# Two bias rows of a graph network's node stage: added on GpSimd's prepared rows, or by a rank-two product on TensorE

## What is computed

```
x = _layernorm(h + o, ln1_g, ln1_b)
f = jax.nn.relu(x @ W1 + b1) @ W2 + b2
return _layernorm(x + f, ln2_g, ln2_b)
```

## Time and profile before

| | |
|---|---|
| median of 3 runs | 2845.94 us (2825.38 to 2848.08) |
| the profiled execution | 2843.35 us, its span 2841.2 us |
| granted TensorE clock, mean of the span | 0.889 |
| busy: TensorE, VectorE, ScalarE, GpSimd | 2310.8, 1811.9, 1010.0, 1152.9 us |
| L335, L338 | 160 matmul passes each (two for each product), from 121.8 to 1017.5 us |

### The profile page before, as it was taken

The page is one execution under the profiler, slowest core; times in us unless marked ns, Lnnn a source line. Parts: engine busy times, 40 slices in busy tenths (PEclk is TensorE's granted clock), DMA queues, the critical chain, the costliest instruction groups (busy, mean ns, idle before and its releaser), DMA issues.

```text
span 2841.2 us, 29188 instructions
## 1 busy us (share of the span) xinstructions
PE 2310.8 (81%) x9582; PEld 1207.5 (42%) x9582; DVE 1811.9 (64%) x3780; ACT 1010.0 (36%) x1735; POOL 1152.9 (41%) x869
## 2 busy tenths in 40 slices
PE   8589999999999859999056766639999798398887
PEld 4245555555545435545022122114444554154465
DVE  2999887888887872245763443363566748647753
ACT  2134545455445442121152222231111132256554
POOL 1777445363767264320626556531120201133222
PEclk9799999999999989999568888769899698599988
DMA  6324333433344146325645565571120202223221
GB/s 196 92 76 117 119 101 115 114 116 116 104 123 114 51 117 164 100 76 172 193 144 141 149 170 137 155 215 46 44 71 17 77 10 58 72 71 81 56 56 52
DMA packets 214465, 298.37 MB, mean 105 GB/s; under 512 B 99951, under 2 KB 100446, under 8 KB 212957
## 3 DMA queue, kind: packets, MB, share of 16 engines
q1 hardware_dynamic: 108116, 213.88, 25.1%
q0 software_dynamic: 106240, 83.12, 11.8%
HBM read 171.56 MB, written 160.65 MB: 117 GB/s over the span
## 4 chain that ended last, share of the span: by engine, by line
PE 56%; DVE 19%; issue 7%; POOL 6%; DMA 6%; ACT 4%; SPq 1%; POOLq 0%; DVEq 0%; ACTq 0%
PE bank L1939 8%; PE bank L321 7%; PE bank L938 7%; PE bank L305 6%; POOL arena L1532 4%; PE bank L2535 3%; PE bank L297 3%; DVE Bd L592 3%; PE bank L918 3%; DMA arena<-y_table,ids 2%; PE bank L312 2%; POOL arena L1030 2%; PE bank L313 2%; PE bank L2418 2%; DVE st L605 2%
## 5 line engine op out<-in xcount | busy, mean ns | idle before, releaser
L1030 POOL DMA_INDIRECT arena<-x_table,idd x120 | 150.5, 1254 | 649.8 <-DVE arena L2205 155.8
L305 PE MATMUL bank<-arena 128*125 128x512 f32 x640 | 292.8, 612 | 15.3 <-DMA ident<-ident_in 8.8
L1586 PE MATMUL bank<-arena 125*125 125x512 f32 x360 | 213.2, 725 | 106.5 <-DMA arena<-y_table,ids 98.5
L1939 PE MATMUL bank<-arena 128*125 128x512 f32 x640 | 292.3, 611 | 1.4 <-DVE Md L2159 0.7
L1532 POOL DMA_INDIRECT arena<-y_table,ids x180 | 228.6, 1270 | 155.7 <-DMA y_table<-arena 103.6
L321 PE MATMUL bank<-arena 128*125 128x512 f32 x640 | 278.5, 593 | 2.1 <-ACT arena L486 1.8
L1760 DVE SCALAR_TENSOR_TENSOR arena<-arena,v,bank 125x512 f32<-125x512 f32 x180 | 134.4, 747 | 193.9 <-PE bank L1586 180.6
L748 POOL TENSOR_TENSOR arena<-arena,rowv 125x512 f32<-125x512 f32 x80 | 100.3, 1286 | 356.4 <-DVE arena L676 314.3
L946 ACT ACTIVATE arena<-bank 128x500 f32<-128x500 f32 (+1 forms) x210 | 114.9, 589 | 293.5 <-PE bank L918 144.0
L938 PE MATMUL bank<-arena 128*125 128x512 f32 x480 | 208.7, 593 | 0.0
L1637 ACT ACTIVATE bank<-arena 125x512 f32<-125x512 f32 x180 | 107.5, 600 | 269.0 <-DVE arena L1760 256.3
(11 more groups left out here) (398 smaller groups left out, 4331.2 us busy)
## 6 DMA issues: line engine op xcount, KB each, us to landing
y_table<-arena SPq DMA_DIRECT2D x36, 896.0 KB
p_table<-arena SPq DMA_DIRECT2D x25, 896.0 KB
z_table<-arena SPq DMA_DIRECT2D x25, 896.0 KB
x_table<-arena SPq DMA_DIRECT2D x25, 896.0 KB
arena<-x_cols SPq DMA_DIRECT2D x20, 1000.0 KB
arena<-x SPq DMA_DIRECT2D x20, 896.0 KB
out<-arena SPq DMA_DIRECT2D x20, 896.0 KB
x_by_src<-arena SPq DMA_DIRECT2D x5, 896.0 KB
```

What stands on the lines that cost most here:

```text
L305: i = nc.tensor.matmul(b[0:P, :], xT[:, k, j * P:(j + 1) * P], W1r[:, k, :], start=k == 0, stop=k == KC - 1)
L1030: nc.gpsimd.indirect_dma_start(out=dst, out_offset=None, in_=table, in_offset=bass.IndirectOffsetOnAxis(ap=idx, axis=0), bounds_check=limi ...
L1586: nc.tensor.matmul(bank[t % RING1][0:P, :], Ss[:, t, :], V1[:, t, :], start=False, stop=True, skip_group_check=True).then_inc(P_sum, 1)
L1939: i = nc.tensor.matmul(b[0:P, :], fT[:, k, j * P:(j + 1) * P], W[:, k, :], start=k == 0, stop=k == KC - 1)
```

## The change

The products of L338 are gone, and the four small loads of their two rows with them. A row `ffn_b` (ln1_b and b2 broadcast to 125 partitions by two loads, added once by VectorE at the end of step 0) is added by GpSimd to U, between L750 and L754. L748 now counts on a new semaphore `tm`, and the addition counts on `tg`, for which VectorE's L655 waits. The rows of ones stay for other uses.

```diff
@@ sp_second_loads
-            for dst, src in ((wleft, w_left), (w2x4[:, 0, :], w_ffn[:, 0:D])):
+            for dst, src in ((wleft, w_left), (w2x4, w_ffn)):
                 sp.dma_start(dst, src).then_inc(s_w2, 16)
-            for j in range(TG):
-                sp.dma_start(w2x4[32 * j:32 * j + 2, 1, :], w_ffn[0:2, D:2 * D]).then_inc(s_w2, 16)
@@ pe_step
                 for j in range(TG):
-                    nc.tensor.matmul(bs[j][0:P, :], f1T[32 * j:32 * j + 32, :], w2x4[32 * j:32 * j + 32, 0, :],
-                                     start=True, stop=False)
-                for j in range(TG):
-                    nc.tensor.matmul(bs[j][0:P, :], ones4[32 * j:32 * j + 2, :], w2x4[32 * j:32 * j + 2, 1, :],
-                                     start=False, stop=True).then_inc(NR_ps, 1)
+                    nc.tensor.matmul(bs[j][0:P, :], f1T[32 * j:32 * j + 32, :], w2x4[32 * j:32 * j + 32, :],
+                                     start=True, stop=True).then_inc(NR_ps, 1)
@@ pool_step
                 for j in range(TG):
-                    nc.gpsimd.tensor_tensor(U[:, j, :], T[1 - par][:, j, :], row(R_LN1G), ALU.mult).then_inc(B["tg"], 1)
+                    nc.gpsimd.tensor_tensor(U[:, j, :], T[1 - par][:, j, :], row(R_LN1G), ALU.mult).then_inc(B["tm"], 1)
                 for j in range(TG):
                     nc.gpsimd.tensor_scalar(T[1 - par][:, j, :], T[1 - par][:, j, :], q2[1 - par][:, j:j + 1], None,
                                             ALU.mult).then_inc(B["wq"], 1)
+                for j in range(TG):
+                    pool.wait_ge(B["tm"], 4 * nB + j + 1)
+                    nc.gpsimd.tensor_tensor(U[:, j, :], U[:, j, :], ffn_b, ALU.add).then_inc(B["tg"], 1)
@@ SyncE, step 0
                     sp.dma_start(rowv[:, R_LN1G:R_END, :], rows[R_LN1G:R_END].partition_broadcast(P)).then_inc(s_rows, 16)
+                    for dst, r in ((ffn_b, R_LN1B), (ffn_b2, R_L2B2)):
+                        sp.dma_start(dst, rows[r].partition_broadcast(P)).then_inc(s_rows, 16)
@@ VectorE, behind its step 0
+                    if s == 0:
+                        dve.wait_ge(s_rows, 16 * 3)
+                        nc.vector.tensor_tensor(ffn_b, ffn_b, ffn_b2, ALU.add).then_inc(wp_rdy, 1)
@@ GpSimd, ahead of its step 1
-                    pool.wait_ge(s_rows, 16)
+                    pool.wait_ge(s_rows, 16 * 3)
+                    pool.wait_ge(wp_rdy, 3)
```

More of the change, by code:

```diff
@@ L105, in gnn_kernel @@
         kd = at(23848, [2, 2 * ET], P)
-        w2x4 = at(35499, [2, D])
+        w2x4, ffn_b = at(35499, [D]), at(34907, [D], P)
+        ffn_b2 = at(23928, [D], P)
         WM0, maps, ones4 = at(36523, [128]), at(36651, [M_END, 128]), at(37675, [P])
@@ L123, in gnn_kernel @@
         B = {k: sem("B_" + k) for k in
-             "tg wq w bn ag sc rt rc ug z3 bn3 ag3 sc3 rt3 rc3 x3".split()}
+             "tm tg wq w bn ag sc rt rc ug z3 bn3 ag3 sc3 rt3 rc3 x3".split()}
         C = {k: sem("C_" + k) for k in
@@ L345, in pe_step @@
                 if isinstance(s, int) and s == 1:
-                    pe.wait_ge(s_w2, 16 * 7)
+                    pe.wait_ge(s_w2, 16 * 3)
                 pe.wait_ge(A["t"], 4 * s)
@@ L1865, in sp_L2 @@
             sp.dma_start(RD[:, :, :], RSd.rearrange("(t p) q -> p t q", p=P)).then_inc(rec_back, 16)
-            sp.wait_ge(s_w2, 16 * 9)
+            sp.wait_ge(s_w2, 16 * 5)
             sp.dma_start(C3[:, 0:M_NDC, :], maps_d[:, 0:M_NDC * 128]).then_inc(w2_in, 16)
@@ L2915, in step @@
                 if isinstance(s, int):
+                    if s == 0:
+                        dve.wait_ge(s_rows, 16 * 3)
+                        nc.vector.tensor_tensor(ffn_b, ffn_b, ffn_b2, ALU.add).then_inc(wp_rdy, 1)
                     if s == W_STEP:
                         dve.wait_ge(NT_sb, st_.count("w_g", 1))
-                        dve.wait_ge(s_rows, 16)
-                        dve.wait_ge(s_w2, 16 * 7)
+                        dve.wait_ge(s_rows, 16 * 3)
+                        dve.wait_ge(s_w2, 16 * 3)
                         nc.vector.tensor_copy(maps[:, M_ND1, :], wcol(W_ND1, 128))
@@ L3001 @@
     w32[:, V_F2:V_END] = np.tile(np.concatenate([f2, s2, a["L3_gnn_W_f1"]], axis=1), (4, 1))
-    w_ffn = np.concatenate([np.tile(a["L2_gnn_W2"], (4, 1)), np.zeros((128, D), f32)], axis=1)
-    w_ffn[0, D:], w_ffn[1, D:] = a["L2_gnn_ln1_b"], a["L2_gnn_b2"]
+    w_ffn = np.tile(a["L2_gnn_W2"], (4, 1))
     g2T = a["L3_gnn_W_g2"][:, 0:128].T
```

## The result

The changed kernel takes 2883.35 us (median of 4 runs, 2874.75 to 2901.97) against 2844.93 us before (4 runs): a ratio of 1.0158, 95% interval 1.009 to 1.0227. That is slower, since the interval lies above 1, and by 38 us where 17 were forecast. The profiled execution took 2874.75 us, its span is 2873.0.

The account below looks back on a forecast made before the run. TensorE was taken to bound the loop, with VectorE's route only 1.4 us behind. 9.5 (steady) + 3.7 (first) + 4 (last) = 17 us on 2843.35 gave 2860.5, as median 2863 us; own range 2852 to 2876.

Parts of the forecast that it names:

- wider range: Whole kernel: 2835 to 2892 us, from a partial gain to long waits in nearly all steps.
- second rival: Loop steps: L704 or L711 waits to the train's end, 2879 us for half the steps, 2895 for all; chance 0.2.
- TensorE's part: Loop steps: dropping the products of L338 takes 0.97 us off TensorE per step, at most 19 us over twenty steps.
- Where the train lies: Loop steps: L754 moves into L741's place, L741 4.9 us later over VectorE's L725, L726 and L728, making VectorE's route longer.
- the price of a blocked L704: Loop steps of the other parity: L704 waits for one L754 instruction, about 1.2 us more, making the step 47.0 us.
- steady part: Loop steps: 0.45 or 1.65 us longer in turn, 8.4 us for eight, 1 for a late one; +9.5 us.
- The clock: TensorE in the loop: left out as the clock showed 1.00; a fall in the new gaps would make the sum wrong.
- First steps: Up to step 3: loads 2.0, counting passes 3.5, a blocked L704 1.2, L671 relieved by 3; sum +3.7 us.
- Last steps: Where records are built: four small VectorE copies take 1.2 us each, +4 us; the four steps after taken as 0.
- The 0.97 us come out: Loop steps: small operations slip in between the new instructions and TensorE sets the step; 2827 to 2843 us, chance 0.2.
- Nothing happens: Whole kernel: TensorE spends the products' time anyway and port costs cancel; within 5 us of 2846, chance 0.1.
- The blocked operations wait to the end of a longer train: Loop steps: L704 gets in only after 9.8 us of GpSimd instructions, making a step 49.5 us, 4.1 longer; chance 0.2.

Follow-up runs that it names:

- e1_no_bias: The changed kernel without its four additions on GpSimd, both bias rows left out of the result: 2838.19 us, ratio 0.9997 to the kernel before.
- e8_drained: The changed kernel with each instruction of GpSimd's trains L737, L750 and L753 waiting for the end of the one before it: 2862.85 us, ratio 1.01.
- e9: The changed kernel with L737 held until VectorE's first L608 of the step, and pauses between the instructions of GpSimd's trains: 2845.36 us, ratio 0.9991.
- e10: The kernel before with its L741 held until VectorE's first L612 of the step, and pauses between the instructions of GpSimd's trains: 2821.88 us, ratio 0.9922.
- e5_apart: The changed kernel with, from step 4 on, L753 moved into the next step behind the first L608, and L737 behind L655: 2841.94 us, ratio 1.001.
- e2_both: The kernel before with the two loads and four GpSimd additions of a row of zeros added, TensorE's products kept: 2888.16 us, ratio 1.0187.

## Why the prediction was right in direction and short in size

The kernel became slower, as forecast, but 2883 us lies above the forecast's own range of 2852 to 2876 and within the wider range that made room for the second rival. In the node stage the trace shows 42.3 us for the forecast's 17: 32.5 in steps 4 to 13 (forecast 9.5), 4.4 before them (3.7) and 5.5 behind (4).

**TensorE's part.** Forecast 0.97 us per step, measured 0.86 (45.41 to 44.55 us, e1_no_bias). The mechanism was right, and so was the claim that VectorE would take the gain away: of the nine steps 5 to 13 two reach 45.3 and 45.4 us, none less.

**Where the train lies.** Right: L753 in L737's old place, and L737 over L722 and L724, which take 0.88 and 1.30 us in steps 5, 7 and 11, as forecast (0.8 to 1.3); in steps 6, 10 and 13 only L722 is long, and in the others L700 has already waited to the train's end, or nearly. And in six of the nine steps TensorE stands still ahead of its first gate product for 2.4 to 3.7 us (forecast 1 to 3), released by ScalarE's evacuation.

**The term that was mis-sized** is the price of a blocked L704 (now L700) in a loop step. I took "one instruction of L754, about 1.2 us more", with steps of 45.8 and 47.0 us in turn and +9.5 us for the steady part. It was +24.1 us in steps 5 to 13 and +8.4 in step 4. In steps 4, 8, 9 and 12 L700 waited 10.63, 5.60, 5.80 and 7.57 us, three of them to the end of the whole L737 train. That is my second rival, which had 0.2 and 2879 us for half of the steps. The forecast loop exists: it is that of e8_drained from step 7 on, where every wait is one instruction, with steps of 46.6 us (forecast mean 46.4). Its ratio of 1.010 is to a kernel before without pauses, which gain time there too.

The evidence was there. The L704 of the earlier trace rows waited from 679.72 to 682.31, and L741 ended at 677.31 + 4.97 = 682.28: it, too, had waited to the end of a train, which was then only two instructions away; so had the L704 of steps 7, 9 and 11. I read it as a number of instructions instead of as a place. The Trainium skill ("SBUF — State Buffer", Who interferes with whom) says that whichever of the two issues first has the shared ports for a whole instruction and the other blocks. e8_drained agrees: 1.32 us at the most in these steps, and a GpSimd instruction takes 1.24. Without pauses the rule is short of what the runs show, nine instructions in step 4; what the lone instruction costs is one thing, who gets the ports at its end another. I had let that rule count against the rival.

**The clock.** I left it out, and named it as something that could spoil the sum. It did, by nearly half of what steps 5 to 13 lost. Windows of TensorE in the changed kernel (busy, granted clock, DMA share, GB/s), behind the idle time of step 6 and behind that of step 12:

```profile
350.13:353.13 3.00, 0.91 (x9) 1.00 0.84 189
353.13:356.13 3.00, 2.70 (x4) 0.52 0.96 335
```

```profile
637.40:640.40 3.00, 0.92 (x9) 1.00 0.83 197
640.40:643.40 3.00, 2.70 (x7) 1.00 0.96 298
```

After 2.39 us of idle time in step 6 TensorE runs at 0.52, the 1.2 GHz level, for some 3 us; after 2.38 us in step 12 it stays at 2.4 GHz. From L311 to the last a_o2 bank (fourth L615) the one takes 376.98 - 353.43 = 23.55 us, the other 662.66 - 640.70 = 21.96:

```profile
353.43 2.03 PE L311 MATMUL bank<-arena,ws 128*128 128x500 f32 x2 [2.39 <-ACT arena L482]
```

```profile
376.98 0.69 DVE L615 TENSOR_TENSOR arena<-arena,bank 125x512 f32<-125x512 f32 x1 [2.75 <-PE bank L320]
...
662.66 0.69 DVE L615 TENSOR_TENSOR arena<-arena,bank 125x512 f32<-125x512 f32 x1 [2.74 <-PE bank L320]
```

So 1.6 us for each such step. Steps 6, 8, 9, 10 and 13 show it, 8 of the 24.1 us, and step 4 does. Step 5 begins at the lower level, behind 5.16 us of idle time that the 10.63 us of L700 brought, and comes to its first transposes (L296) 2.9 us later than step 6 does (10.92 against 8.04 us from its start), so some 11 of the 24.1 us are clock:

```profile
287.50:292.50 5.00, 0.01 (x1) 0.93 0.01 2
292.67:295.67 3.00, 3.00 (x9) 0.50 0.18 16
295.67:298.67 3.00, 3.00 (x5) 0.51 0.92 285
298.67:301.67 3.00, 3.00 (x8) 1.00 0.23 49
```

Gaps of 1.8 us or less (e8_drained, step after step) left the clock at 1.00. A gap's length alone doesn't decide: behind 2.33 us in step 4 of e8_drained the clock stayed at 1.00 too, behind 2.08 us in step 4 of the changed kernel it fell. These waits on VectorE were thus paid twice, once as a gap and once as slow products behind it.

**First steps.** Forecast +3.7, measured +4.4, but by other terms, so the agreement is luck. The window of 28 to 42 us moved 223 GB/s, not 255, and the counting began 1.2 us later (78.11 against 76.92), not 2.0; the step 2 product came 4.7 us later, which the "5 us later" of the forecast meets. Step 2, with +1.2 forecast, is 4.1 us shorter, as L704 had waited 5.54 us there and L700 takes 0.55. Step 3 is 3.8 us longer: the three microseconds that L671 was to give back there didn't come, it takes 8.12 us for four, hardly less than the 8.52 of the earlier trace rows.

```profile
78.11 0.35 DVE L588 SCALAR_TENSOR_TENSOR Bd<-Sd,kfc,arena 125x125 uint8<-125x125 f32 x1
...
197.40 8.12 DVE L667 SCALAR_TENSOR_TENSOR arena<-arena,nb,rowv 125x512 f32<-125x512 f32 x4
```

**Last steps.** The record copies were forecast at +4 us, and step 14 is 5.5 us longer; more operations in the records' row take 1.2 us each (L1095 to L1103), and L1109 2.39 us for two copies:

```profile
761.81 2.39 DVE L1109 COPY Md<-kfc 125x20 f32<-125x20 f32 x2
...
781.15 4.79 DVE L608 TENSOR_SCALAR sr<-mv 125x4 f32<-125x4 f32 x1
```

For steps 15 to 18 I had taken 0; they came to -3.8, and the L612 of the earlier trace rows met the train again, with 4.79 us. Step 19, which I had not named, is 4.8 us longer. In both kernels most of these steps are longer than they need be, through waits that fall here or there. e9 and e10 show what the additions cost when the longest of these are gone: 15 us in steps 14 to 20, where GpSimd also writes the records.

**The rivals.** "The 0.97 us come out" is refuted for this placement, and shown to be true for another (e5_apart, 44.55 us in every loop step). "Nothing happens" is refuted by the interval. "The blocked operations wait to the end of a longer train" happened in three of the ten loop steps, and in a fourth (step 4) nearly to its end. **The chances**: 0.67 stood on a change under 1% and it was 1.6%; 0.28 stood on slower by more.

**What stays open** is what decides, in a train without pauses, whether VectorE gets in at the next boundary (steps 5 to 7, 10, 11, 13) or only later (4, 8, 9, 12). The pauses show what removes the long wait, not what chooses between the two. Where in a GpSimd instruction the small operation starts doesn't decide it alone: in e2_both L705 (L700) starts 1.08 us into one in steps 8 and 10, and takes 0.23 and 7.56 us. Nor does a long wait always last to the end of a train: besides the L700 of step 4, L608 there waits 8.32 us (258.88 to 267.20) and gets in between L744 and L746, which follow without a pause.

## What to carry to other kernels

Before work is put on GpSimd, ask which small VectorE operations on the critical chain will find it busy, and price each at the whole run of back-to-back GpSimd instructions that may follow, not at one. A hold that starts the train behind the chain's small operations, or a wait between its instructions, costs one line and is worth trying by itself: here it gave 0.5 to 0.8% without the change, as much as the change could have given at its best (19 us). Give the kernel before the same hold when the two are compared; otherwise its gain is booked to the change. And where the bounding engine would get gaps like those here (2 to 5 us), look at its granted clock behind them before calling the gap the whole price.

## What the hardware showed beyond expectation

- A VectorE operation on 125x4 numbers, 0.17 us alone, took up to 13.3 us beside GpSimd's trains (e2_both, step 4), and a counting pass of some 1.3 us took 11.48 us in the kernel before. RECIPROCAL on the same tiles, in the same place, stayed at 0.16 to 0.18 us, and so did additions with a PSUM bank as an input (0.69 us).
- A wait for the instruction before it, though it costs only 0.2 us, ended these long waits of small operations; the counting pass fell to 2.31 us, and a GpSimd instruction there took (8.21 us for four) 2.05 instead of 1.23 us, as if the two engines now took turns.
- TensorE fell to about half its clock for some 3 us behind six of the seven gaps of 2.08 to 3.67 us ahead of its first gate product in steps 4 to 13 of the changed kernel. The exception is the 2.38 us of step 12; and behind the gaps of 1.8 us or less in the loop of e8_drained it never fell.
